# Second mixture of experts: routing weights spread over the partitions by transfers, one half weighted on GpSimd, DVE and ACT steps reordered

## The reference, cut to what matters

```python
def _L2_ffn_ref(hidden_states, gate_w, w_gate, w_up, w_down):
    ...
    logits = x.astype(jnp.float32) @ gate_w.astype(jnp.float32).T
    scores = jax.nn.softmax(logits, axis=-1)
    topk_w, topk_ids = jax.lax.top_k(scores, TOP_K)
    topk_w = topk_w / (topk_w.sum(axis=-1, keepdims=True) + 1e-20)
    ...
    g = jax.lax.ragged_dot(sorted_tokens, jnp.swapaxes(w_gate, 1, 2), group_sizes)
    u = jax.lax.ragged_dot(sorted_tokens, jnp.swapaxes(w_up, 1, 2), group_sizes)
    h = jax.nn.silu(g) * u
    out = jax.lax.ragged_dot(h, jnp.swapaxes(w_down, 1, 2), group_sizes)
    ...
    y = (unsorted.reshape(B * S, TOP_K, D) * topk_w[..., None]).sum(axis=1)
```

## Time and profile before

| what | value |
|---|---|
| time, median of 3 runs | 763.48 us (759.99 to 767.42) |
| the profiled execution: its own time | 768.57 us |
| its span in the profile | 766.8 us |
| mean granted TensorE clock | 0.881 |
| busy over the span | PE 631.2 us, DVE 577.2, ACT 361.5, POOL 325.7 |
| the mixture's chunks, first gate matmul to last down matmul | from 399.46 us to about 611.3 us |

### The profile page before, as it was taken

One profiled execution on the slowest core, in us unless ns is written; L12 is line 12 of the kernel. 1 busy time (PEld: TensorE's weight loads), 2 busy tenths in 40 slices (PEclk: granted clock), 3 DMA queues, 4 the chain that ended last, 5 costly groups with the idle time before them and its releaser, 6 DMA issues.

```text
span 766.8 us, 16854 instructions
## 1 busy us (share of the span) xinstructions
PE 631.2 (82%) x5168; PEld 306.5 (40%) x5168; DVE 577.2 (75%) x1160; ACT 361.5 (47%) x665; POOL 325.7 (42%) x581
## 2 busy tenths in 40 slices
...
DMA packets 42196, 25.78 MB, mean 34 GB/s; under 512 B 13161, under 2 KB 41073, under 8 KB 42018
## 3 DMA queue, kind: packets, MB, share of 16 engines
q1 hardware_dynamic: 40594, 23.00, 10.6%
...
## 4 chain that ended last, share of the span: by engine, by line
PE 67%; DVE 19%; POOL 4%; issue 3%; ACT 3%; DMA 2%; SPq 1%; DVEq 0%; POOLq 0%; ACTq 0%
PE PS L195 54%; DVE SHARED L1162 3%; DVE MB L1196 2%; PE PS L1284 2%; PE PS L1175 2%; PE PS L1290 2%; DMA WF<-in_wsmall 2%; DVE MF L1196 1%; PE PS L1249 1%; DVE REC L1298 1%; DVE XN L341 1%; PE PS L565 1%; PE PS L1227 1%; ACT SHARED L527 1%; POOL RSTD L337 1%
## 5 line engine op out<-in xcount | busy, mean ns | idle before, releaser
L921 ACT ACTIVATE SHARED<-SHARED 128x512 f16<-128x512 f32 x180 | 113.3, 630 | 121.5 <-DVE SHARED L933 116.3
L939 DVE TENSOR_TENSOR SHARED<-SHARED 128x512 f16<-128x512 f32 x180 | 140.3, 782 | 35.1 <-ACT SHARED L921 34.4
L195 PE MATMUL PS<-XH,UH 128*128 128x512 f16 x296 | 114.9, 388 | 2.2 <-ACT CT L744 2.2
L195 PE MATMUL PS<-XL,UH 128*128 128x512 f16 x296 | 114.8, 388 | 0.0
L195 PE MATMUL PS<-XH,UL 128*128 128x512 f16 x296 | 114.5, 387 | 0.0
L195 PE MATMUL PS<-SHARED,DNH 128*128 128x512 f16 x360 | 107.1, 379 | 5.4 <-DVE SHARED L939 5.3
L1267 ACT ACTIVATE SHARED<-PS 128x512 f32<-128x512 f32 x96 | 52.4, 595 | 100.4 <-PE PS L195 75.4
L930 DVE TENSOR_TENSOR SHARED<-SHARED,PS 128x512 f32<-128x512 f32 x116 | 78.6, 678 | 12.5 <-PE PS L195 12.5
L852 POOL CAST DNH<-DF 128x128 f16<-128x128 f32 x90 | 31.4, 349 | 126.3 <-PE PS L195 126.3
L933 DVE TENSOR_TENSOR SHARED<-SHARED,PS 128x512 f32<-128x512 f32 x116 | 79.7, 687 | 4.0
L842 POOL TENSOR_TENSOR UL<-UF,UH 128x256 f16<-128x256 f32 (+1 forms) x90 | 72.9, 810 | 7.2
...
## 6 DMA issues: line engine op xcount, KB each, us to landing
...
WF<-in_wsmall SPq DMA_DIRECT2D x1, 808.0 KB, 12.8
X<-in_x SPq DMA_DIRECT2D x1, 512.0 KB, 3.8
```

The source lines that it names most:

```text
L195: last = pe.matmul(dst, l, r, start=start and i == 0, stop=stop and i == len(pairs) - 1)
L921: act.activation(HHI[:, u, hf, :], (HF if M["gated"] else RH[u])[:, hf, :], ACT.Copy).then_inc(sem("e_high"), 1)
L939: dve.tensor_tensor(HLO[:, u, hf, :], src[:, hf, :], HHI[:, u, hf, :], ALU.subtract).then_inc(sem("e_low"), 1)
```

## The change

After `route_dve` has made LE, PE turns LE itself in float32 (8 transposes, 64 x 512 in each of two banks), ACT copies both halves to WROWS (64 x 1024, SBUF), SP stores WROWS in DRAM (256 KB) and, for every chunk, reads rows of it back with a broadcast into one of two buffers WB (128 partitions x 1024 tokens, 512 KB a chunk, in two transfers, one for each expert of the chunk). The weight matmul, SEL and its load, and the two casts L778 and L779 are gone from this mixture.

In a chunk, half 0 is now weighted first: POOL multiplies SG by WB into TG (`moe1_pool_weigh`), DVE multiplies TG by up from PSUM into HF (`moe1_dve_first`). Half 1: DVE multiplies SG by up from PSUM into TG (`moe1_dve_gate`) and TG by WB into HF (`moe1_dve_second`), whose inputs both lie in SBUF. DVE's order is gate 1, first 0, second 1, low 0, low 1. ACT's is silu 0, high 1 of the chunk before, silu 1, high 0. POOL's is weigh of chunk c, up split of chunk c + 2, down split of chunk c + 1. SP's is WB of chunk c, up of c + 2, down of c + 1. PE does gate and up of chunk 0 before the turning of LE, without waiting for the routing.

The thirteen loads of ACT at the start, but for the first two, share one semaphore (`ld_late`), and each wait on one of them becomes a wait on all eleven; these waits stand in stages after the loads. In the third mixture POOL waits for the up matmuls in place of the weight matmul.

The diff, cut to the mixture:

```diff
...
+        WB = [piece(at, 1024) for at in (8192, 9216)]
+        WROWS = piece(10240, 1024, parts=E2)
...
+            if m == 1:
+                logits = bank(6)[:, 0:NB * E].rearrange("p (b e) -> p b e", b=NB)
...
             last.then_inc(sem("r_logits"), 1)
-            pe.wait_ge(sem("r_weights"), m + 1)
+            if m == 1:
+                return
+            pe.wait_ge(sem("r_weights"), m // 2 + 1)
...
-                step(dve.tensor_tensor(le, le, along(ZS[:, 3, :], E), ALU.mult))
-                step(dve.tensor_copy(CW[:, :, 0:E], le))
-                dve.tensor_tensor(CW[:, :, E:2 * E], le, CW[:, :, 0:E], ALU.subtract).then_inc(sem("r_weights"), 1)
+                dve.tensor_tensor(le, le, along(ZS[:, 3, :], E), ALU.mult).then_inc(sem("w1_weights"), 1)
...
-                    pool.wait_ge(sem("e_weight"), 2 * (M["gat"] + c) - 2)
+                    pool.wait_ge(sem(f"e_up{m}"), 2 * c - 2)
...
             products(pe, bank(hf), three(UH[:, u, 0:128], UL[:, u, 0:128], XHh[hf], XLh[hf])).then_inc(sem("e_gate"), 1)
             if M["gated"]:
-                if not (isinstance(ga, int) and ga == 0):
+                if m == 1 and not (isinstance(c, int) and c == 0):
+                    if hf == 0:
+                        pe.wait_ge(sem("w1_first"), c)
+                    else:
+                        pe.wait_ge(sem("w1_gated"), c)
+                if m == 2 and not (isinstance(ga, int) and ga == 0):
                     pe.wait_ge(sem("e_gated"), 2 * ga + hf - 1)
                 products(pe, bank(2 + hf), three(UH[:, u, 128:256], UL[:, u, 128:256], XHh[hf], XLh[hf]))\
-                    .then_inc(sem("e_up"), 1)
-            if not M["gated"]:
+                    .then_inc(sem(f"e_up{m}"), 1)
+            if m < 2:
                 return
...
-                if not (isinstance(c, int) and M["gat"] + c == 0):
-                    act.wait_ge(sem("e_gated"), 2 * (M["gat"] + c) + hf - 1)
+                if not (isinstance(c, int) and c == 0):
+                    if m == 2:
+                        act.wait_ge(sem("e_gated"), 2 * c + hf - 1)
+                    elif hf == 0:
+                        act.wait_ge(sem("w1_weighed"), c)
+                    else:
+                        act.wait_ge(sem("w1_gated"), c)
                 act.activation(SG[:, hf, :], bank(hf), ACT.Silu).then_inc(sem("e_act"), 1)
...
-            if M["gated"]:
-                act.wait_ge(sem("e_hidden"), 2 * (M["gat"] + c) + hf + 1)
+            if m == 1:
+                act.wait_ge(sem("w1_second" if hf else "w1_first"), c + 1)
+            elif m == 2:
+                act.wait_ge(sem("e_hidden"), 2 * c + hf + 1)
...
+        def moe1_pool_weigh(pool, c, u, h):
+            pool.wait_ge(sem("e_act"), 2 * (CH0 + c) + 1)
+            pool.wait_ge(sem(f"w1_in{u}"), 32 * h + 32)
+            if not (isinstance(c, int) and c == 0):
+                pool.wait_ge(sem("w1_first"), c)
+            pool.tensor_tensor(TG[:, 0, :], SG[:, 0, :], WB[u][:, 0:HALF], ALU.mult).then_inc(sem("w1_weighed"), 1)
+        def moe1_dve_first(dve, c):
+            dve.wait_ge(sem("w1_weighed"), c + 1)
+            dve.wait_ge(sem("e_up1"), 2 * c + 1)
+            dve.wait_ge(sem("e_low"), 2 * (CH0 + c) - 1)
+            dve.tensor_tensor(HF[:, 0, :], TG[:, 0, :], bank(2), ALU.mult).then_inc(sem("w1_first"), 1)
+        def moe1_dve_gate(dve, c):
+            dve.wait_ge(sem("e_act"), 2 * (CH0 + c) + 2)
+            dve.wait_ge(sem("e_up1"), 2 * c + 2)
+            if not (isinstance(c, int) and c == 0):
+                dve.wait_ge(sem("w1_second"), c)
+            dve.tensor_tensor(TG[:, 1, :], SG[:, 1, :], bank(3), ALU.mult).then_inc(sem("w1_gated"), 1)
+        def moe1_dve_second(dve, c, u, h):
+            dve.wait_ge(sem("w1_gated"), c + 1)
+            dve.wait_ge(sem(f"w1_in{u}"), 32 * h + 32)
+            dve.wait_ge(sem("e_low"), 2 * (CH0 + c))
+            dve.tensor_tensor(HF[:, 1, :], TG[:, 1, :], WB[u][:, HALF:TOK], ALU.mult).then_inc(sem("w1_second"), 1)
+        SPANS = (((0, 96, 0), (96, 128, 1)), ((0, 64, 1), (64, 128, 2)), ((0, 32, 2), (32, 128, 3)))
...
+        def moe1_sp_weights(sp, c, ex, k):
+            if not (isinstance(c, int) and c < 2):
+                sp.wait_ge(sem("w1_first"), c - 1)
+                sp.wait_ge(sem("w1_second"), c - 1)
+            for lo, hi, j in SPANS[k % 3]:
+                settled(sp, "sp")
+                sp.dma_start(WB[k % 2][lo:hi, :], t["w1"][bass.ds(ex + j, 1), :].to_broadcast([hi - lo, TOK]))                    .then_inc(sem(f"w1_in{k % 2}"), 16)
+        def moe1_sp(sp):
+            moe1_sp_up(sp, 0, 0)
+            moe1_sp_up(sp, 1, 1)
+            moe1_sp_down(sp, 0, 0)
+            sp.wait_ge(sem("w1_rows"), 2)
+            sp.dma_start(t["w1"], WROWS).then_inc(sem("w1_out"), 16)
+            sp.wait_ge(sem("w1_out"), 16)
+            def step(c, ex, k, up=True, down=True):
+                moe1_sp_weights(sp, c, ex, k)
+                if up:
+                    moe1_sp_up(sp, c + 2, k % 2)
+                if down:
+                    moe1_sp_down(sp, c + 1, 1 - k % 2)
+            with sp.Fori(1, CH2 // 6 - 1) as i:
+                for k in range(6):
+                    step(6 * i + k, 8 * i + 4 * (k // 3), k)
...
+        def moe1_pool(pool):
+            moe_pool_up(pool, 1, 0, 0, 0)
+            moe_pool_up(pool, 1, 1, 1, 0)
+            moe_pool_down(pool, 1, 0, 0, 0)
+            def step(c, u, h, up=True, down=True):
+                moe1_pool_weigh(pool, c, u, h)
+                if up:
+                    moe_pool_up(pool, 1, c + 2, u, h + 1)
+                if down:
+                    moe_pool_down(pool, 1, c + 1, 1 - u, h + u)
+            with pool.Fori(1, CH2 // 2 - 1) as i:
+                step(2 * i, 0, i)
+                step(2 * i + 1, 1, i)
...
+        def moe1_rows_pe(pe):
+            pe.wait_ge(sem("w1_weights"), 1)
+            for b in range(NB):
+                last = pe.transpose(bank(4 + b // 4)[0:E2, 128 * (b % 4):128 * (b % 4) + 128], LE[:, b, :], EYE[:])
+                if b % 4 == 3:
+                    last.then_inc(sem("w1_turned"), 1)
+        def moe1_rows_act(act):
+            for i in range(2):
+                act.wait_ge(sem("w1_turned"), i + 1)
+                act.activation(WROWS[:, HALF * i:HALF * i + HALF], bank(4 + i)[0:E2, :], ACT.Copy).then_inc(sem("w1_rows"), 1)
...
+                if m == 1 and isinstance(c, int) and c == 0:
+                    moe1_rows_pe(pe)
...
-                for hf in range(2):
-                    moe_act_silu(act, m, c, u, hf)
-                for hf in range(2):
-                    moe_act_high(act, m, c, u, hf)
+                moe_act_silu(act, m, c, u, 0)
+                if m == 1 and not (isinstance(c, int) and c == 0):
+                    moe_act_high(act, 1, c - 1, 1 - u, 1)
+                moe_act_silu(act, m, c, u, 1)
+                if m == 1 and isinstance(c, int) and c == 0:
+                    moe1_rows_act(act)
+                moe_act_high(act, m, c, u, 0)
+                if m == 2:
+                    moe_act_high(act, m, c, u, 1)
             chunks(act, m, step)
+            if m == 1:
+                moe_act_high(act, 1, n - 1, 1, 1)
             act.wait_ge(sem("e_down"), 2 * (MOE[m]["at"] + n))
             act.activation(YS[:], bank(6, 2), ACT.Copy).then_inc(sem("y_out"), 1)
...
+                if m == 1:
+                    moe1_dve_gate(dve, c)
+                    moe1_dve_first(dve, c)
+                    moe1_dve_second(dve, c, u, h)
+                else:
+                    for hf in range(2):
+                        moe_dve_hidden(dve, m, c, u, hf)
...
+    t["w1"] = nc.dram_tensor("w1_rows_dram", (E2, TOK), mybir.dt.float32, kind="Internal").ap()
...
```

More of the change, by code:

```diff
@@ L823, in moe_sp @@
                 return
-            if not (isinstance(c, int) and M["gat"] + c < 2):
-                sp.wait_ge(sem("e_weight"), 2 * (M["gat"] + c) - 2)
+            if not (isinstance(c, int) and c < 2):
+                sp.wait_ge(sem("e_weight"), 2 * c - 2)
             settled(sp, "sp")
```

77 lines of the change are left out of this document (50 added, 27 removed).

## The result

The changed kernel takes 788.24 us (median of 4 runs, 785.08 to 790.44) against 762.65 (4 runs, 759.99 to 767.42): a ratio of 1.0325, 95% interval 1.0262 to 1.0389, slower. The profiled execution took 788.11 us, its span is 786.3, its clock 0.894.

What follows compares the result with a forecast made beforehand. PE bounds the kernel before at 4.32 us a chunk; the port shared by DVE and POOL would bind at 4.70. Steady +17.5, start +3.8, end -0.6 sum to +20.7: 784 us from the median 763.48, range 772 to 804.

Steps and rivals of the forecast that it cites:

- The steady part: 46 chunks after the first two, each going from 4.32 to 4.70 us: +17.5 us, bounds +9.2 and +35.
- the end: Between the last up and the last down, one DVE multiply less: -0.6 us.
- PE's 3.89: In a chunk, PE loses two of 20 matmuls: 18 x 0.216 = 3.89 us.
- rival 1: In the steady chunks the port does not bind and PE does: 747 us, faster; chance 0.10.
- The exclusion of the port: DVE instructions with both inputs in SBUF and POOL instructions reading SBUF exclude each other for their whole length.
- The sum is 4.52: Port time in a chunk: DVE's second 1 and low parts 1.83, POOL's work 2.69, in sum 4.52 us.
- 0.18 of idle: Time the port stands free in a chunk, added to 4.52 to give 4.70 us.
- the record minus 0.07: Each instruction holds the port until 0.07 us before its record ends.
- This is no worse than PE: The chunk's ring first 0, high 0, silu 0, high 1, low 1, gate 1 takes 3.89 us, as PE does.
- The start: From LE to chunk 2's gate, with turning, store, broadcast and first matmuls: 16.4 against 12.7 us, +3.8, bounds +2 to +6.
- What the profile would show: Mixture chunk 4.7 us, PE gaps some 0.8 a chunk, POOL nearly always busy, weigh not waiting for a DMA.
- L988 was to rise to 0.9 and more: DVE's second 1 in the mixture, lengthened by blocking, together with low part L1071, to 0.9 us and more.

Runs made afterwards that it cites:

- e3: The changed kernel without POOL's weigh, so half 0 stays unweighted: 740.94 us, chunk 3.89 us.
- e1: The changed kernel with WB broadcast for chunks 0 and 1 only and then kept: 789.58 us, chunk 4.73 us.
- e9: The changed kernel with ACT's order of the kernel before (silu 0, silu 1, high 0, high 1): 770.16 us, chunk 4.35 us.
- e2: The changed kernel with second 1 reading PSUM in place of WB, so half 1 is not weighted: 778.65 us, chunk 4.44 us.

## Why the prediction was right, and where it was not

**The sign and the size.** Forecast 784 us, measured 788.24, within the range. Against the kernel before, +20.7 was forecast, and the stretch grew by 23.1. The steady part was forecast at +17.5 and the end at -0.6, 16.9; it measured +17.9.

**PE's 3.89.** Right, by e3. The two matmuls saved are real: without weigh the kernel runs at 741 us, near the 747 of rival 1, whose condition was that weigh hold the port for less.

**The exclusion of the port.** Right: blocks of whole instructions stand in every timeline above. With the Trainium skill, page "SBUF — State Buffer", section "Who interferes with whom", which calls the pair of ports that VectorE and GpSimd share an exclusive lock, the trace agrees: low 1 lasted 1.75 in place of 0.68. The same section says that a DMA contends with no compute engine; e1's unchanged 4.73 without the broadcasts agrees. In one point the prediction drew its conclusion narrower than its rows: the scaling L341 of the earlier trace rows, which took 1.41 in place of 0.34 beside POOL's multiplies, has one tile as input and two per-partition scalars, so it is not only instructions with two input tiles that can be blocked.

**"The sum is 4.52", with 0.18 of idle: 4.70.** The number was met (4.72), the working behind it was not; two errors cancelled. First, the port is held for less than the record minus 0.07. What fits the timelines is that an instruction that waited ends its record its own length less 0.07 after the holder let go, and itself lets go 0.07 before that end, so in a row of handovers each costs about its record less 0.14. Read from the timeline of the changed kernel, from let go to let go, the eight of a chunk are: weigh 1.19, low 1 0.55, UH 0.25, UL 0.60, second 0.61, DNH 0.15, low 0 0.62, DNL 0.28, in sum 4.25. Second, the port stood free for 0.47 in a chunk, not for 0.18 (0.15 between UH and UL, 0.19 ahead of second 1, 0.09 ahead of low 0, 0.04 ahead of weigh). What holds the chunk at 4.72 all the same is the next point.

**"This is no worse than PE", of ACT's ring.** This step failed. The ring was summed as 3.89, without weigh. No semaphore orders weigh against the low 1 beside it; the port does. The ring that holds the changed kernel is read from its timeline: first 506.94, high 0 507.72, low 0 508.39, weigh 509.33 (behind DNL, which was behind low 0), low 1 behind weigh, and gate 1 of the next chunk with low 1's end at 511.06, 1.73 after weigh began (one chunk earlier 504.61 to 506.34), and first 0.60 after that: 0.78 + 0.67 + 0.94 + 1.73 + 0.60 = 4.72. High 1 stands behind silu 0 and so comes 0.06 too late for low 1 to take the port ahead of weigh. e9 takes only this away, and 17.8 of the 23.1 us go; e3 takes only weigh away, and the new ACT order costs nothing. So the steady loss against the kernel before needs both, weigh in the port and ACT's new order. Second 1 in the port adds to it: without it (e2) the same order gives 4.44. A forecast for e9 by the prediction's own method would have been 4.7 or more (mine was 4.6 to 4.9), and wrong.

**The start, +3.8 forecast, +5.3 measured.** Mis-sized in two terms. The store took 3.06 where 2.5 was taken (and 2.7 was called the most), the broadcast 5.20 where 3.8 + 0.3 was taken; 5.5 had been named as its limit. The turning with its copy (2.62 for 2.7), weigh and first (2.04 for 1.94) and the matmuls at the low clock (5.02 for 5.2) were right.

**What the profile would show.** Chunk, PE's gaps (26.9 us in 40 chunks, 0.67 each), POOL's share, weigh waiting for no DMA, clock 1.00: as said. Wrong: L988 was to rise to 0.9 and more; it stayed at 0.68 in every chunk, because it comes when POOL has just finished UL and the next cast comes 0.03 behind it. All of DVE's blocking fell on the second low part, 1.75. Who is blocked is a matter of the order of arrival, and I had spread it evenly.

**Open.** Whether the port alone, with an order that never lets it idle, would go below e9's 4.35 was not tried; the held times read above, 4.25, would be its floor, against PE's 3.89.
